# Attention with expert routing on one core: probability-times-V products in two column groups of 64, with three steps of the tile order moved

## What is computed

```python
h = layernorm(x) * (1 + ca) + sa
scores = einsum('bhncd,bhnkd->bhnck', qc, kc) * SCALE        # 64 queries, 128 keys
attn = softmax(where(mask, scores, -inf))
out = einsum('bhnck,bhnkd->bhncd', attn, vc)                 # the products of this change
x = x + ga * (out @ w_out.T)
h = layernorm(x) * (1 + cb) + sb
probs = softmax(abs(u * silu(g)));  w, idx = top 4 of probs + extra_bias
x = x + gb * (sum over the 4 experts of w * expert(h) + shared(h))
```

## Time and profile before

| what | value |
|---|---|
| runs | 573.96, 574.01, 567.19 us, median 573.96 |
| profiled execution | span 566.3 us from the first to the last instruction |
| what lies around the span | no time of its own is given for that execution; the lowest run, 567.19, is 0.9 above its span |
| granted TensorE clock, mean over the span | 0.950 |
| attention, 84 to 270 us | TensorE busy 176.25 of 186, clock 1.00 |
| VectorE, ScalarE, GpSimd busy over the span | 396.3, 284.1, 291.9 us |

### The profile page before, as it was taken

One profiled execution on the slowest core, in us unless ns is written; L12 is line 12 of the kernel. 1 busy time (PEld: TensorE's weight loads), 2 busy tenths in 40 slices (PEclk: granted clock), 3 DMA queues, 4 the chain that ended last, 5 costly groups with the idle time before them and its releaser, 6 DMA issues. The chain is left out here.

```text
span 566.3 us, 12354 instructions
## 1 busy us (share of the span) xinstructions
PE 492.5 (87%) x3575; PEld 464.1 (82%) x3575; DVE 396.3 (70%) x1099; ACT 284.1 (50%) x743; POOL 291.9 (52%) x330
## 2 busy tenths in 40 slices
PE   2699999999999999998430488999999999999996
PEld 0589998999999898988330377999999999999995
DVE  6769953456867768687763798867777776784575
ACT  2368754554554545533262564555655655553331
POOL 6446603010346446465766799544444444446994
PEclk9999999999999999999555599999999999999999
DMA  7457996779747456422858443343434444356951
GB/s 196 134 170 217 254 307 205 196 206 229 209 125 216 139 164 183 124 86 83 267 203 271 135 132 103 116 136 119 140 120 127 132 124 137 119 158 249 413 204 74
DMA packets 62982, 98.00 MB, mean 173 GB/s; under 512 B 9747, under 2 KB 48210, under 8 KB 61574
## 3 DMA queue, kind: packets, MB, share of 16 engines
q1 hardware_dynamic: 50664, 57.80, 37.8%
q0 software_dynamic: 9136, 32.53, 15.2%
q10 hardware_dynamic: 3118, 6.89, 3.9%
HBM read 60.49 MB, written 40.04 MB: 178 GB/s over the span
## 5 line engine op out<-in xcount | busy, mean ns | idle before, releaser
L1702 POOL DMA_INDIRECT ys_scr<-h,ids_st x59 | 61.0, 1033 | 67.4 <-DVE h L1756 63.9
L140 POOL DMA_INDIRECT xs_scr<-h,slot_u x64 | 62.9, 982 | 54.0 <-PE TB L1302 26.6
L105 PE MATMUL GU<-gu_hi,xT 128*128 x316 | 84.1, 348 | 1.9 <-DVE xT L1736 1.9
L1626 ACT ACTIVATE aT<-HT 88x256 fp32r<-88x256 f32 (+1 forms) x95 | 37.8, 399 | 65.9 <-PE HT L1862 65.9
L105 PE MATMUL YP<-dn_hi,aT 88*128 x316 | 67.1, 304 | 4.4 <-DVE aT L1741 3.9
L1748 DVE TENSOR_TENSOR h_act<-GU,g_act 128x176 f32<-128x176 f32 (+1 forms) x95 | 35.2, 371 | 46.4 <-ACT g_act L1619 46.2
L919 ACT ACTIVATE prob<-TB 128x512 f32<-128x512 f32 x64 | 38.2, 597 | 56.5 <-PE TB L1302 55.8
L1312 PE MATMUL O<-raw,prob 128*128 128x99 f32 x512 | 66.2, 275 | 0.0
L1312 PEld LDWEIGHTS O<-raw,prob 128*128 128x128 f32 x512 | 61.6, 192 | 0.1
L105 PEld LDWEIGHTS YP<-dn_hi,aT 88*128 88x128 f32 x316 | 47.5, 188 | 11.1 <-issue 7.5
L105 PEld LDWEIGHTS GU<-gu_hi,xT 128*128 128x128 f32 x316 | 52.1, 192 | 2.3 <-issue 2.3
(11 more groups left out here) (243 smaller groups left out, 1252.8 us busy)
## 6 DMA issues: line engine op xcount, KB each, us to landing
x_st<-xs_scr SPq DMA_DIRECT2D x79, 144.0 KB
dn_hi<-k_scr SPq DMA_DIRECT2D x48, 192.0 KB, 3.8
planes<-ys_scr POOLq DMA_DIRECT2D x8, 1024.0 KB, 17.1
k_scr<-raw SPq DMA_DIRECT2D x8, 768.0 KB, 6.1
dn_hi<-q_scr SPq DMA_DIRECT2D x24, 256.0 KB, 4.4
q_scr<-raw SPq DMA_DIRECT2D x8, 512.0 KB, 3.6
raw<-in_egu SPq DMA_DIRECT2D x8, 352.0 KB
raw<-in_x SPq DMA_DIRECT2D x16, 128.0 KB, 4.0
```

The lines of the kernel that those rows point to most:

```text
L105: mm = eng.matmul(out, a, b, start=(i + j == 0), stop=(i == len(pairs) - 1 and j == 2))
L140: eng.indirect_dma_start(T["xs_scr"], bass.IndirectOffsetOnAxis(ap=T["slot_u"][:, par, t % 2, k:k + 1], axis=0), T["h2"][:, row, :], None) ...
L1626: eng.activation(aT[0:rows, p2, 0, 0:k, :], HT[p2][0:rows, 0:k * P].rearrange("p (k x) -> p k x", k=k), ACT.Copy).then_inc(aT_hi, 1)
L1702: eng.indirect_dma_start(ys, bass.IndirectOffsetOnAxis(ap=ids_st[:, r:r + 1].bitcast(U32), axis=0), results(r % 8), None).then_inc(sent[q] ...
```

## The change

`weigh` sends each head's product twice, for c = 0 and c = 1: 64 columns of the stationary matrix each, into output partitions 0 to 63 and 64 to 127. The moving matrix is the same 99 columns both times. Three steps change places in the order of a tile: `scores_t(n, t, 2)` goes ahead of `weigh(n, 0)`, `weigh(n, 1)` goes ahead of `transpose_max`, and `ranks` goes ahead of `weigh(n, 2)`. No wait, buffer or DMA changes.

```diff
             for hh in range(4):
                 head = 4 * q + hh
                 at = (head % 8) * VC
-                mm = eng.matmul(O[:, head // 8, at:at + WIDE * VC], prob[:, q, hh * P:(hh + 1) * P],
-                                VW[:, bass.ds(HEADS * n + head, WIDE), :].rearrange("p h x -> p (h x)"), start=True, stop=True)
+                for c in range(2):
+                    mm = eng.matmul(O[c * CH:(c + 1) * CH, head // 8, at:at + WIDE * VC],
+                                    prob[:, q, hh * P + c * CH:hh * P + (c + 1) * CH],
+                                    VW[:, bass.ds(HEADS * n + head, WIDE), :].rearrange("p h x -> p (h x)"), start=True, stop=True)
             mm.then_inc(pv_mm, 1)
...
                 transpose_o(m)
+            scores_t(n, t, 2)
             weigh(n, 0)
-            scores_t(n, t, 2)
+            weigh(n, 1)
             if more and n >= 1:
                 eng.wait_ge(oT_lo, m + 1)
                 transpose_max(n1, (t + 1) % 2)
-            weigh(n, 1)
             if runs(n, 1):
                 if more:
                     eng.wait_ge(mt_cp, n + 2)
                 project_out(m)
             scores_t(n, t, 3)
-            weigh(n, 2)
             if not even and runs(n, 5):
                 ranks(e - 2, par, X)
+            weigh(n, 2)
             weigh(n, 3)
```

## The result

The changed kernel took 578.93 us (median of four runs, 577.25 to 580.57), the kernel before beside it 573.99 (four runs, 567.19 to 575.41). The ratio is 1.0135, 95% interval [1.008, 1.019]: slower, but within the 2% that a measurement here can tell. In a later set of runs, with the kernel before at 568.87, the ratio was 1.0187 [1.0157, 1.0217]. A ratio is made from fast runs, those within 1.5% of the fastest of their kernel, while a median is that of all runs, so the two can differ (the medians here give 1.0086). The forecast was 579.5, range 569 to 606, "within 2%" the likeliest; it came right.

What follows compares the result with a forecast made beforehand. Attention was taken as bound by TensorE, with VectorE's chain bounding odd tiles. Nine even tiles at +0.27 and six odd at +0.51 gave +5.5 us on the median of 573.96: 579.5, range 569 to 606.

Steps and rivals of the forecast that it cites:

- Even tile: Attention tile from rden to rden, nine counted: `project_out` must wait for the copy of mT; +0.27 us a tile.
- The count of the kinds: Attention's tiles: nine counted as even, tiles 1 to 4 included for having no ranks, and six as odd.
- Odd tile: Attention tile with ranks, six counted: the ranks await msum and both groups stand behind them; +0.51 us a tile.
- w = 0.80: Microseconds of TensorE for one `weigh` group of four heads after the change, between stream and load bounds; before 0.90.
- s = 0.05: Microseconds per block of groups for changing to the narrower form and back, judged from the 16-column transposition.
- the lower bound that I had from the stream: A `weigh` group with both halves streaming side by side and loads hidden: 0.68 us, +0.8 us in all.
- Serial: Rival in `weigh`: the two halves stream one behind the other, 1.36 us a group; +31.5 us, 605.5; chance 0.17.
- fixed beat: Rival in `weigh`: each pass keeps 0.111 us whatever its width, 1.79 us a group; +55 us, 629; chance 0.08.
- The drain at a switch: Rival: TensorE drains at each change of form, 0.165 us each; +6.7 us on top, 586.2; chance 0.10.
- The faster rival: Rival in `weigh`: loads and streams of both halves side by side, 0.45 us a group; -4.1 us, 569.9; chance 0.08.
- w = 0.94: Cost of a `weigh` group, in us, from which on the prediction called the kernel slower than before.
- The clock: Rival: new waits ahead of `project_out` and the ranks bring a low-clock stretch into attention; some 50 us, 630; chance 0.05.

Runs made afterwards that it cites:

- ranks_back: The changed kernel with the ranks put back between `weigh` 2 and 3; 571.79 us, ratio to the kernel before 1.0031 [0.9991, 1.0071].
- s3_last_split: The changed kernel with `scores_t` 3 ahead of `project_out` and the ranks behind `weigh` 3; median 573.30 us, ratio to the kernel before 0.9911.
- split_only: The kernel before, its old order kept, with only the products narrowed to 64 columns; 573.29 us, ratio to the kernel before 1.0109.

## Why the prediction came right

**Even tile.** Right, step by step. From the load of `scores_t` 2 to the transposition 2.34 (209.79 to 212.13), forecast 2.35. The copy of mT exposed: 0.64, forecast 0.61. From `project_out` to rden 3.25 (212.77 to 216.02), forecast 3.42. From rden to `scores_t` 2 5.91, where I took it unmoved at 5.76: the way out of `weigh` 3 now lies behind rden. Together +0.28 against +0.27. The last two stretches were off by 0.17 and 0.15 in opposite ways, so that the sum agrees so closely is luck. It holds for tiles 4, 8 and 10. The count of the kinds was wrong: tiles 1 to 3 don't behave like even ones, nor tile 5 like the other odd ones.

**Odd tile.** Right: +0.45 against +0.51. The transposition still waits for o_lo, the ranks start 0.05 behind msum (226.06 + 0.17, load at 226.28), and both groups stand behind them. `ranks_back` shows that this place decides it.

**The group's cost, two sizes that cancelled.** I took w = 0.80 a group and s = 0.05 for a form's change and back. Two groups' starts span 1.34 us, sixteen pairs some 0.085 apart but for a first step of 0.136, so 0.68 a group: the lower bound that I had from the stream, not the mean between stream and load. The ways in and out cost more. Matmuls of 128 columns start 0.11 apart at the boundary; into the narrower form it is 0.20, and out of it 0.18 where 0.05 stood:

```profile
232.88 1.98 PE L1312 MATMUL O<-raw,prob 128*128 128x99 f32 x16
234.64 0.48 PE L1287 MATMUL SB<-mask_key,mask_qry 126*128 126x512 f32 x1
```

In before, above, the last product starts at 232.88 + 1.98 - 0.27 = 234.59 and the next at 234.64. In `s3_last_split`:

```profile
218.70 1.59 PE L1313 MATMUL O<-raw,prob 128*64 128x99 f32 x32
220.22 0.28 PE L1352 MATMUL X<-mask_e,tri 128*128 128x16 f32 x1
```

the last starts at 218.70 + 1.59 - 0.25 = 220.04 and the next 0.18 later (0.05 at the same place in before). That is 0.21 us a block for both ways, four times my s. The two errors cancelled: I had a block of two groups shrink from 2 x 0.90 to 1.65, by 0.15, and from the start ahead of it to the start behind it the block went from 1.87 to between 1.70 and 1.73, by 0.14 to 0.17 (1.79 where the second group awaits prob 3). A lone group costs 1.02 to 1.04 in place of 0.92 to 1.01, a pair of groups some 1.72 in place of 1.87: that is why the narrower products lose in the old order, which has lone groups, and gain in the new one.

**The rivals.** Serial and fixed beat fell with the pairs. The drain at a switch was half right: there is a gap at each one, of 0.21 for both ways and not 0.33, and my sum for it kept w = 0.80, so 586.2 was too dear. The Trainium skill, TensorEngine Tiling (Array Packing), Key Properties, names such a drain. The trace agrees that the change to the 64-column form and back costs time, against my reading of the earlier trace rows, but not that the engine runs empty: the first O product starts 0.20 behind a matmul that lasts 0.27. The 16-column transposition shows nothing above 0.05. I shouldn't have taken the one narrower form for the other. The faster rival needed w = 0.45; the stream bounds at 0.68.

Two readings in that list don't follow from its sums: w = 0.94 is where the sum passes 2%, not where the kernel becomes slower, and no sum stands under the 0.03 for faster by over 2%.

**The clock.** Wrong in form, and this is the step of the prediction that failed. I had it as all or nothing, 50 us with a chance of 0.05, since waits of 1.30 us had left the clock at 1.00. It comes in pieces of 3.4 us that cost a tile 1 to 2 us, four of them in the profiled execution, and in other kernels here in longer ones, up to 20.5 us. By my own signs ("a granted clock below 1 before 270 us") that rival came, at a fraction of its price. That the number stands is in part luck: the tiles grew by some 4.2 rather than 5.5, the clock took a share that the sum had not, and the median I added to, 573.96, probably held such pieces already. Against before at 568.87 in the later set, the difference is 9.9 us, more than the sum: the tiles' 4.2 and, as far as the profiles tell, the clock.

## What to carry to other kernels

Price a reordering by what stands between a producer and its consumer: here two steps moved by one place each (`scores_t` 3 in even tiles, the ranks in odd ones) were worth 0.6 us a tile, more than the change of the instruction itself. Products parted into column groups are worth it only in long blocks, with the groups interleaved pass by pass; count 0.2 us for every block that they make. Once a wait is gone, look for the next one: the better orders ran into GpSimd and a DMA. A new wait may also cost through the clock, so look at the granted clock behind each new wait, and compare kernels by medians of many runs and by their tiles, not by one pair of profiles.

## What the runs showed of the hardware

- Two column groups of 64 stream at the same time with float32 of 99 columns: a pair every 0.085 us, where a pass of 128 columns took 0.111.
- By the rhythm of the starts, products of the other column group start out of program order: with all of one half first, the second half's first matmul began with three passes of the first still to come, 0.397 us into the block.
- Going from 128-column products to 64-column ones and back costs 0.09 and 0.12 us beyond the usual 0.11 and 0.05; the first narrower one starts 0.20 behind a matmul that lasts 0.27.
- The granted clock fell to 0.50 in the midst of attention, for 3.4 us behind stretches in which TensorE was busy for 1.99 to 2.32 of 3.40 us, and also behind ones in which it was busy for all 3.40; in other kernels for 6.8 and 20.5 us. The same kernel waited in other tiles without a fall, and the kernel before has falls in some executions only. What decides it stays open.
- Two VectorE operations that take 0.29 and 0.17 us in most tiles took 2.00 and some 1.06 in the last one, in after as in `split_only`. What holds them there no run shows.
